# A graph network of four layers: own rows transposed and joined on VectorE in the first stage, b2 added as a product on TensorE in the second

## The reference, cut to what matters

```python
def gcn_layer(x, edge_index, W, b, num_nodes):
    src, dst = edges + self loops
    deg  = segment_sum(ones, dst)
    dinv = rsqrt(deg)
    h    = x @ W
    out  = segment_sum(h[src] * dinv[src] * dinv[dst], dst)
    return out + b
h   = relu(gcn_layer(x, edges, W1, b1))     # 128 -> 256
out = gcn_layer(h, edges, W2, b2)           # 256 -> 128
x   = layernorm(x + out)
```

## Time and profile before

| | us |
|---|---|
| median of 3 runs | 5544.85 (5539.6 to 5549.26) |
| the profiled execution, its own time | 5548.76 |
| its span, first to last instruction | 5547.0 |
| TensorE busy | 4744.4 (86%) |
| VectorE busy | 3861.5 (70%) |
| ScalarE busy | 2782.1 (50%) |
| GpSimd busy | 3017.4 (54%) |

### The profile page before, as it was taken

One profiled execution on the slowest core, in us unless ns is written; L12 is line 12 of the kernel. 1 busy time (PEld: TensorE's weight loads), 2 busy tenths in 40 slices (PEclk: granted clock), 3 DMA queues, 4 the chain that ended last, 5 costly groups with the idle time before them and its releaser, 6 DMA issues. The chain is left out here.

```text
span 5547.0 us, 105377 instructions
## 1 busy us (share of the span) xinstructions
PE 4744.4 (86%) x27509; PEld 3749.1 (68%) x27509; DVE 3861.5 (70%) x11930; ACT 2782.1 (50%) x6703; POOL 3017.4 (54%) x2962
## 2 busy tenths in 40 slices
PE   4499996666799989999999997898799999447887
PEld 4488885555688867777777775777566666227887
DVE  8577775776688855555555554788688888885766
ACT  3644444656333322222222222788677777793545
POOL 0077765777677743333334333777466664007776
PEclk9999998777899989999999998999899999558999
DMA  4889994554577754444444443788877775784554
GB/s 149 274 246 275 273 270 142 151 147 147 177 237 238 236 170 151 153 154 150 150 147 153 152 153 92 223 250 249 245 221 222 222 225 181 261 294 132 153 148 141
DMA packets 551178, 1075.23 MB, mean 194 GB/s; under 512 B 110995, under 2 KB 118202, under 8 KB 547962
## 3 DMA queue, kind: packets, MB, share of 16 engines
q1 hardware_dynamic: 451194, 854.46, 46.5%
q0 software_dynamic: 99840, 219.14, 16.0%
HBM read 712.24 MB, written 360.98 MB: 193 GB/s over the span
## 5 line engine op out<-in xcount | busy, mean ns | idle before, releaser
L841 POOL DMA_INDIRECT s_rows<-t_h,s_index x416 | 525.4, 1263 | 831.5 <-DVE s_index L834 730.5
L841 POOL DMA_INDIRECT cb_rows<-t_x,cb_index x416 | 395.7, 951 | 451.4 <-DVE cb_index L834 327.7
L841 POOL DMA_INDIRECT g_rows<-t_x,g_index x416 | 425.9, 1024 | 384.9 <-issue 366.5
L841 POOL DMA_INDIRECT at_rows<-t_m,at_index x416 | 435.6, 1047 | 299.1 <-DVE at_index L834 189.8
L841 POOL DMA_INDIRECT s_rows<-t_v,s_index x416 | 405.1, 974 | 211.4 <-issue 120.4
L841 POOL DMA_INDIRECT s_rows<-t_x,s_index x416 | 420.5, 1011 | 154.8 <-issue 117.9
L841 POOL DMA_INDIRECT g_rows<-t_h,g_index x416 | 403.1, 969 | 171.1 <-issue 124.7
L905 PE MATMUL bank<-s_onehot,s_hi 128*128 128x80 f32 (+9 forms) x1758 | 436.7, 288 | 48.8 <-DVE s_lo L876 26.6
L1724 DVE TENSOR_TENSOR s_rout<-bank,s_x 128x512 f32<-128x512 f32 x98 | 67.9, 693 | 587.1 <-PE bank L1668 587.1
L905 PE MATMUL bank<-g_onehot,g_rows 128*128 128x80 f32 (+9 forms) x1172 | 299.6, 420 | 199.5 <-DMA g_rows<-t_h,g_index 193.5
L905 PE MATMUL bank<-s_onehot,s_lo 128*128 128x80 f32 (+9 forms) x1758 | 431.0, 285 | 0.0
(11 more groups left out here) (334 smaller groups left out, 13011.1 us busy)
## 6 DMA issues: line engine op xcount, KB each, us to landing
s_scale<-inv_d SPq DMA_DIRECT2D x196, 256.0 KB
t_h<-s_hout SPq DMA_DIRECT2D x98, 512.0 KB
s_own<-t_h SPq DMA_DIRECT2D x98, 512.0 KB
t_m<-s_mout SPq DMA_DIRECT2D x98, 264.0 KB
at_own<-t_m SPq DMA_DIRECT2D x98, 264.0 KB
t_x<-so_x SPq DMA_DIRECT2D x98, 256.0 KB, 4.7
g_own<-t_x SPq DMA_DIRECT2D x98, 256.0 KB
g_scale<-dinv_d SPq DMA_DIRECT2D x98, 256.0 KB
```

What stands on the lines that cost most here:

```text
L841: pool.indirect_dma_start(out=self.rows[:, self.ring(q) + k, :], out_offset=None, in_=self.table[0:NPAD, :], in_offset=bass.IndirectOffset ...
```

## The change

In `gcn_first` the own rows are no longer added by products. TensorE transposes them (`flip`, last in its step, for group s) into bank 6 or 7, ScalarE copies them out (`turn`, for s-1, into four buffers `own_t`), and VectorE joins them with the sums: own times `own1` plus the bank, then in a second instruction times the row of `dinv`. Since banks 6 and 7 are taken, the first product has one pair of banks (2 and 3) and waits for the ReLU of the group before. The addition of b2 leaves VectorE's `rest`. In `gcn_second` the four transposes become products with the identity, each followed in the same bank by a product of the root of the degree (one row of 128 nodes) with b2 (one row): scaled by `dinv` afterwards, that is b2. For this the roots are kept as a third row table `root_d`, and SyncE loads 2 KB of it for each group, before the load of `r1`. `scale_degrees` and `scale_x` run for unsorted inputs only.

```diff
@@ sort_and_scale
-                sp.wait_ge(copied, 2)
+                sp.wait_ge(copied, 3)
                 sp.dma_start(dinv_d, rows[0]).then_inc(kept_d, 16)
                 sp.dma_start(inv_d, rows[1]).then_inc(kept_d, 16)
-                sp.wait_ge(kept_d, 32)
+                sp.dma_start(root_d, rows[2]).then_inc(kept_d, 16)
+                sp.wait_ge(kept_d, 48)
...
-                for i, tile in enumerate((dinv_n, inv_n)):
+                for i, v in enumerate((by_group(dinv_n), by_group(inv_n), root)):
...
-                for i in range(2):
+                for i in range(3):
                     dve.tensor_copy(rows[i], bank[2 + i][0:T, :]).then_inc(copied, 1)
@@ gcn_first, sync
-                    (0, lambda q: load(sp, q, own_rows[q.u][:, :], own_group(t_x0, q.t), loaded[q.u], e.summed)),
+                    (0, lambda q: load(sp, q, own_rows[q.u][:, :], own_group(t_x0, q.t), loaded[q.u], owned)),
@@ gcn_first, tensor
                 def sums(q):
                     e.fetched(pe, q)
+                    if not is_first(q.t):
+                        pe.wait_ge(agged, q.t - 1)
+                    e.sum_by_feature(pe, q, [bank[q.u]]).then_inc(e.summed, 1)
+
+                def flip(q):
                     pe.wait_ge(loaded[q.u], q.n * 16 + 16)
                     if not is_first(q.t):
-                        pe.wait_ge(agged, q.t - 1)
-                    e.sum_by_feature(pe, q, [bank[q.u]], close=False)
+                        pe.wait_ge(turned, q.t - 1)
                     for b in range(BLK):
-                        last = pe.matmul(nodes(bank[q.u])[:, b, :], own_rows[q.u][:, b * D:(b + 1) * D],
-                                         id_own1[:, :], start=False, stop=(b == BLK - 1),
-                                         skip_group_check=True)
-                    last.then_inc(e.summed, 1)
+                        last = pe.transpose(bank[6 + q.u][:, b * P:(b + 1) * P],
+                                            own_rows[q.u][:, b * D:(b + 1) * D], ident[:, :])
+                    last.then_inc(owned, 1)
 
                 def up(q):
                     pe.wait_ge(agged, q.t + 1)
-                    if not is_first(q.t):
-                        pe.wait_ge(relued, q.t - 1)
+                    if not (isinstance(q.t, int) and q.t < 1):
+                        pe.wait_ge(relued, q.t)
                     for h in range(2):
-                        last = pe.matmul(bank[2 + 4 * q.u + h][:, :], w1_s[:, h * P:(h + 1) * P], agg[q.u][:, :],
+                        last = pe.matmul(bank[2 + h][:, :], w1_s[:, h * P:(h + 1) * P], agg[q.u][:, :],
                                          start=True, stop=True)
...
-                over_groups(pe, [(1, sums), (5, down), (3, up)])
+                over_groups(pe, [(1, sums), (5, down), (3, up), (0, flip)])
@@ gcn_first, scalar
+                def turn(q):
+                    act.wait_ge(owned, q.t + 1)
+                    if not is_first(q.t, 4):
+                        act.wait_ge(agged, q.t - 3)
+                    act.activation(own_t[q.r][:, :], bank[6 + q.u][:, :], ACT.Copy).then_inc(turned, 1)
...
-                over_groups(act, [(4, relu), (6, scale), (0, lambda q: e.take_hi(act, q))])
+                over_groups(act, [(4, relu), (6, scale), (1, turn), (0, lambda q: e.take_hi(act, q))])
@@ gcn_first, vector
                 def scale_sums(q):
+                    dve.wait_ge(turned, q.t + 1)
                     dve.wait_ge(e.summed, q.t + 1)
+                    if not is_first(q.t):
+                        dve.wait_ge(hidden, q.t - 1)
+                    dve.scalar_tensor_tensor(out=planes(agg[q.u]), in0=planes(own_t[q.r]), scalar=own1[:, 0:1],
+                                             in1=nodes(bank[q.u]), op0=ALU.mult, op1=ALU.add).then_inc(link, 1)
+                    dve.wait_ge(link, q.t + 1)
                     dve.wait_ge(loaded_s[q.u], q.n * 16 + 16)
-                    if not is_first(q.t):
-                        dve.wait_ge(hidden, q.t - 1)
-                    dve.tensor_tensor(planes(agg[q.u]), nodes(bank[q.u]), planes(scale_row[q.u]), ALU.mult)\
+                    dve.tensor_tensor(agg[q.u][:, :], agg[q.u][:, :], scale_row[q.u][:, :], ALU.mult)\
                        .then_inc(agged, 1)
...
-                    last.then_inc(link, 1)
-                    dve.wait_ge(link, q.t + 1)
-                    dve.tensor_tensor(rout[q.u][:, :], rout[q.u][:, :],
-                                      b2_r[:, :, :].rearrange("p b f -> p (b f)"), ALU.add)\
-                       .then_inc(rested, 1)
+                    last.then_inc(rested, 1)
@@ gcn_second
                 over_groups(sp, [
+                    (3, lambda q: load(sp, q, root_row[q.u][:, :], root_d[bass.ds(q.t, 1), :], loaded_s[q.u],
+                                       turned)),
...
+                    pe.wait_ge(loaded_s[q.u], q.n * 16 + 16)
                     for b in range(BLK):
-                        last = pe.transpose(bank[2 + q.u][:, b * P:(b + 1) * P],
-                                            agg[q.u][:, b * P:(b + 1) * P], ident[:, :])
+                        f = slice(b * P, (b + 1) * P)
+                        pe.matmul(bank[2 + q.u][:, f], agg[q.u][:, f], ident[:, :], start=True, stop=False,
+                                  skip_group_check=True)
+                        last = pe.matmul(bank[2 + q.u][:, f], root_row[q.u][:, f], b2_r[0:1, 0, :], start=False,
+                                         stop=True, skip_group_check=True)
```

More of the change, by code:

```diff
@@ L216, in build_program @@
     inv_d = dram("inv_d", (T, GRP))
+    root_d = dram("root_d", (T, GRP))
     idx = sb("idx", [P, SLOTS], U32)
@@ L362, in sort_and_scale @@
             deg, root = tmp("deg", [P, T, BLK]), tmp("root", [P, T, BLK])
-            rows = [t[:, :, :, :].rearrange("p c o f -> p (c o f)")[0:T, 0:GRP] for t in value]
+            rows = [value[u][:, :, :, :].rearrange("p c o f -> p (c o f)")[0:T, at:at + GRP]
+                    for u, at in ((0, 0), (1, 0), (0, GRP))]
             xin = [tmp(f"x{u}", [P, GRP]) for u in range(AHEAD)]
@@ L511, in _ @@
                 pe.wait_ge(inverted, len(PIECES))
-                for i, tile in enumerate((dinv_n, inv_n)):
+                for i, v in enumerate((by_group(dinv_n), by_group(inv_n), root)):
                     for k in range(BLK):
-                        last = pe.transpose(bank[2 + i][0:T, k * P:(k + 1) * P], by_group(tile)[:, :, k], ident[:, :])
+                        last = pe.transpose(bank[2 + i][0:T, k * P:(k + 1) * P], v[:, :, k], ident[:, :])
                 last.then_inc(flipped, 1)
@@ L1207, in _ @@
                 sp.wait_ge(made, 2)
-                sp.dma_start(dinv_d, root[:, :]).then_inc(kept, 16)
+                sp.dma_start(dinv_d, a[:, :]).then_inc(kept, 16)
                 sp.dma_start(inv_d, b[:, :]).then_inc(kept, 16)
-                sp.wait_ge(kept, 32)
+                sp.dma_start(root_d, root[:, :]).then_inc(kept, 16)
+                sp.wait_ge(kept, 48)
             @block.scalar
@@ L1219, in _ @@
                 pe.wait_ge(made, 2)
-                for i, tile in enumerate((root, b)):
+                for i, tile in enumerate((a, b)):
                     for k in range(BLK):
@@ L1241, in _ @@
                 dve.wait_ge(rooted, 2)
-                then(dve.reciprocal(root[:, :], root[:, :]))
+                then(dve.reciprocal(a[:, :], root[:, :]))
                 dve.memset(bn_mv[:, :], 0.0).then_inc(made, 2)
@@ L1298, in gcn_first @@
             own_rows, xin = ph.pair("own", [P, GRP]), ph.pair("x", [P, GRP])
+            own_t = ph.pair("own_t", [P, GRP], n=4)
             scale_row = ph.pair("scale", [P, GRP])
@@ L1305, in gcn_first @@
             hidden, lowered, link = ph.sem("hidden"), ph.sem("lowered"), ph.sem("link")
+            owned, turned = ph.sem("owned"), ph.sem("turned")
             st_h, st_r = ph.sems("stored_h"), ph.sems("stored_r")
@@ L1367, in relu @@
                     for h in range(2):
-                        last = act.activation(hid[q.u][:, h, :], bank[2 + 4 * q.u + h][:, :], ACT.Relu,
+                        last = act.activation(hid[q.u][:, h, :], bank[2 + h][:, :], ACT.Relu,
                                               bias=b1_c[:, h:h + 1])
@@ L1387, in scale_sums @@
                 def scale_sums(q):
+                    dve.wait_ge(turned, q.t + 1)
                     dve.wait_ge(e.summed, q.t + 1)
-                    dve.wait_ge(loaded_s[q.u], q.n * 16 + 16)
                     if not is_first(q.t):
                         dve.wait_ge(hidden, q.t - 1)
-                    dve.tensor_tensor(planes(agg[q.u]), nodes(bank[q.u]), planes(scale_row[q.u]), ALU.mult)\
+                    dve.scalar_tensor_tensor(out=planes(agg[q.u]), in0=planes(own_t[q.r]), scalar=own1[:, 0:1],
+                                             in1=nodes(bank[q.u]), op0=ALU.mult, op1=ALU.add).then_inc(link, 1)
```

(4 more changed lines are left out.)

## The result

The changed kernel takes 5620.3 us in the median of 4 runs (5613.9 to 5635.9), the kernel before 5542.2 in the median of 4: ratio 1.0139, 95% interval [1.0127, 1.0150]. It is slower by 78 us, where 5524 us had been forecast. The profiled execution took 5616.9 us, its span is 5615.1.

A forecast was written before the change was run, and what follows sets the result against it. TensorE was taken to bound gcn_first, with GpSimd within 3%, and GpSimd gcn_second and sage_first. Gathers -9.5, tail -11.5, sort +0.7 and gcn_second 0 gave -20.3 us: 5524 us, own range 5514 to 5533, full range 5508 to 5540.

The forecast's parts named there:

- gcn_second, TensorE: gcn_second's turn: 16 product instructions at 0.112 us replace four transposes, 1.79 us instead of 0.44, +1.35 a group; cost 0.
- Rival (c): gcn_second: one-partition products don't overlap with the one before, 0.275 us each; TensorE bounds the stage, 5583 us; chance 0.05.
- deciding point: gcn_second: 0.18 us for each of eight one-row instructions, from which TensorE would bound the stage.
- 1.88 free, in which +1.35 fits: gcn_second: TensorE uses 3.52 of 5.40 us a group, so 1.88 us is free for the turn's added 1.35.
- gcn_first, TensorE: gcn_first: 0.98 us of own-row products out, four transposes at 0.11 in; a group falls from 5.84 to 5.30 us.
- 97% that was named as a sign: gcn_first: TensorE busy below 97% would show that the forecast holds.
- The new waits: gcn_first: first product waits for the previous group's ReLU, with 1.9 us of room; own load one step earlier; cost 0.
- gcn_first, GpSimd: gcn_first: index wait of 5.0 us goes, one gather-holding VectorE instruction replaces another; gathers 548 us instead of 557.3, -9.5.
- Tail: gcn_first: time from last gather to the next stage's first falls from 44.6 to 33 us, -11.5; ends 28 and 44.6.
- Sort: End of the sort: a third row store follows the other two, +0.7 us; added transposes and copy are hidden.
- Sum: Whole kernel: -9.5 - 11.5 + 0.7 + 0 = -20.3 us.
- Clock: gcn_second: products replacing transposes raise the granted clock from 0.80, above 0.9 as a sign; counted as 0 us.

The follow-up runs named there:

- the padded kernel: Changed kernel with root row and b2 in tiles of 128 rows, zero except the first, same product order: 5526.2 us, ratio 0.9961 to the kernel before.

## Why the prediction was wrong, step by step

- **gcn_second, TensorE: the step that failed.** "I take the pace, since rows 7 are the same width and type with the weights changed each time." They are, but they also have the same number of rows each time. Every change of it costs 0.19 us at the full clock, eight times a group: the turn takes 3.24 us instead of 1.79. So the cost that was put at 0 was 98 us. With it TensorE needs 6.1 us a group, GpSimd 5.4, and 98 x 0.7 = 69 us, plus 30 of backlog in the tail, are the 98 us. Rival (c) had the effect, at a price of 0.275 for each of the eight one-row instructions (the turn 3.1 us), and the deciding point of 0.18 us an instruction was right; but its cause was the shape of the weights, and the runs show that one row alone goes at 0.112. Its total of 5583 is also added up wrongly: 5545 + 78 - 20 is 5603, nearer to the 5620 measured. 0.05 was far too little for a product of which no row showed the like.
- **"1.88 free, in which +1.35 fits"** was right: the padded kernel does just that, and gcn_second takes 562.7, of which 4.7 us are its first gather.
- **gcn_first, TensorE:** 0.11 for a transpose was right (0.109), and TensorE fell behind GpSimd, though its busy share stayed at 98%, above the 97% that was named as a sign, since durations overlap. The new waits cost TensorE nothing, as said: from 300 to 820 us it waits 7.6 us for VectorE's split rows and 0.7 for nothing that the profile shows, and never for ScalarE.
- **gcn_first, GpSimd:** forecast 548, measured 540.2. Which instructions hold was right: b2's addition, which had held 13.3 us, goes, and the multiply comes. The size was taken from sage_first and does not carry over: there 77 gathers began under the multiply and lost 20.1 us, here 45 began under it and lost 5.6. How often the two meet depends on the order of the stage.
- **Tail:** forecast 33, measured 32.7. It was a choice between 28 and 44.6, and so close a hit is luck; the two padded executions above have 34.6 and 35.6.
- **Sort:** forecast +0.7, measured -2, within what executions differ in: on the chips of the faster kind gcn_first's first gather starts at 253.5 to 260.4 us over twelve traces, and the two of the kernel before are the two ends.
- **Sum:** -20.3 us. The padded kernel, in which the failed step is mended, has -20 us over five rounds. That is partly luck: against before on the same chip gcn_first gives 24 us and gcn_second costs 5, where 21 and 0 had been counted.
- **Clock.** The granted clock of gcn_second rose from 0.80 (0.78 when run again) to 0.84, short of the 0.9 named as a sign, to 0.88 with the products grouped and to 0.93 in the padded kernel; with the transposes kept and no b2 it was 0.77. The rule named in the prediction from the Trainium skill (TensorE: Matmul & The Clock Gate, section on PE-mode transpose) agrees so far; but with b2 in the sums and all transposes kept it was 0.92, so the kind of instruction is not the whole of it.

## What to carry to other kernels

Before a small product is put between big ones on TensorE, look whether its number of rows is theirs. If it isn't, fill it up with zeros, or put all of its kind behind one another where the result allows it (here it did not); 127 rows of zeros cost nothing that the pace of 0.112 us shows, one change costs 0.19. A free stretch on an engine is filled by the pace of what is really between two neighbours, so bound a kind of instruction that no row shows by what it makes of its neighbours too.

## What was not expected of the hardware

- TensorE, f32: 0.112 us from product to product, but 0.205 and 0.213 around a change of the number of rows from 128 to 64, 32 or 1, and 0.200 and 0.213 on the way back.
- TensorE "busy" 500 of 500 us was granted a clock of 0.84, while 360 of 450 without such changes had 0.93: products of 0.33 us on the mean that start 0.2 us apart leave no idle time in such a row.
- VectorE stood still for up to 6.2 us in each of eight passes of a loop, with 41 more instruction packets, and did not with 32 instructions more ahead of the loop.
- The same two kernels order differently by chip: 0.9961 where before takes 5546 us, 1.0112 where it takes 6535. The longer time there is not in the packets, which take 2 to 8% more in all.
